# Scan inputs: centred weight, raw input, one variance per image, first taps on ScalarE, products grouped by form

## The reference

```python
xn = (x - x.mean(1)) / jnp.sqrt(x.var(1) + 1e-5) * ln_w + ln_b   # over the 192 channels, per pixel
xz = jnp.einsum('dc,bchw->bdhw', in_proj_w, xn)                  # 384 x 192
xc, z = jnp.split(xz, 2, axis=1)
xc = conv3x3(xc, conv_w, 'SAME', feature_group_count=192)        # depthwise
xc = silu(xc + conv_b)
x_dbl = jnp.einsum('kcd,bkdl->bkcl', x_proj_w, xs)               # xs: xc read in 4 directions; 12 + 4 + 4 rows each
```

## Time and profile before

| | us |
|---|---|
| median of 3 runs | 5882.74 |
| lowest, highest | 5879.74, 5885.18 |
| span of the profiled execution | 5874.6 |
| busy in the span: PE, DVE, ACT, POOL | 5234.5, 4111.9, 2823.1, 805.7 |

### The profile page before, as it was taken

One profiled execution on the slowest core, in us unless ns is written; L12 is line 12 of the kernel. 1 busy time (PEld: TensorE's weight loads), 2 busy tenths in 40 slices (PEclk: granted clock), 3 DMA queues, 4 the chain that ended last, 5 costly groups with the idle time before them and its releaser, 6 DMA issues. The chain is left out here.

```text
span 5874.6 us, 85825 instructions
## 1 busy us (share of the span) xinstructions
PE 5234.5 (89%) x34692; PEld 2383.9 (41%) x34692; DVE 4111.9 (70%) x4899; ACT 2823.1 (48%) x3955; POOL 805.7 (14%) x826
## 2 busy tenths in 40 slices
PE   7799999999989989968869799989778888888879
PEld 2355555555544434445534333333233333333323
DVE  3477677776621122278878499959789999999963
ACT  1144444444432223245521455526587777867844
POOL 1000000000000011122243100000033333323300
PEclk9899999999999989989989899989889999999999
DMA  6522121221032223344433000013300000000034
GB/s 214 138 39 42 22 42 23 40 43 22 15 110 70 81 77 129 111 142 142 132 119 123 29 29 29 33 47 113 99 29 29 5 28 25 16 29 5 17 113 164
DMA packets 298982, 398.22 MB, mean 68 GB/s; under 512 B 143916, under 2 KB 281316, under 8 KB 295324
## 3 DMA queue, kind: packets, MB, share of 16 engines
q1 hardware_dynamic: 271452, 302.90, 17.6%
q0 software_dynamic: 16096, 73.39, 3.7%
q10 hardware_dynamic: 11040, 16.43, 0.9%
HBM read 226.16 MB, written 166.49 MB: 67 GB/s over the span
## 5 line engine op out<-in xcount | busy, mean ns | idle before, releaser
L3884 DVE TENSOR_TENSOR_SCAN s_h<-s_da,s_h 128x448 f32<-128x448 f32 x672 | 729.6, 1124 | 1.5 <-ACT s_da L3811 1.4
L3731 PE MATMUL s_py<-s_prod,s_idf 128*128 128x448 f32 x1344 | 586.6, 559 | 24.5 <-ACT s_ycol L3824 23.3
L622 PE MATMUL b_pc<-b_ca,b_wdm 128*113 128x392 f32 x1152 | 486.9, 520 | 31.9 <-DVE b_wdm L837 25.8
L3811 ACT ACTIVATE s_da<-s_dt,s_al 128x448 f32<-128x448 f32 x672 | 406.1, 658 | 198.3 <-DVE s_h L3884 147.6
L765 ACT ACTIVATE b_band<-b_psel 124x784 f32<-124x784 f32 x264 | 217.7, 825 | 427.5 <-PE b_psel L690 424.4
L622 PE MATMUL b_pc<-b_cb,b_wdm 128*113 128x392 f32 x960 | 403.0, 520 | 0.0
L3869 DVE TENSOR_TENSOR s_h<-s_dtu,s_pb 128x896 f32<-128x896 f32 x336 | 354.9, 1056 | 31.7 <-POOL s_dtu L3918 23.2
L3891 DVE TENSOR_TENSOR s_prod<-s_h,s_pc 128x896 f32<-128x896 f32 x336 | 360.8, 1074 | 0.1
L3907 POOL TENSOR_TENSOR s_dt<-s_dt,s_dtu 128x448 f32<-128x448 f32 x168 | 249.3, 1484 | 782.7 <-DVE s_h L3884 427.5
L2861 DVE SCALAR_TENSOR_TENSOR j_zc<-j_zt,kept_vec,j_zc 128x896 f32<-128x896 f32 x320 | 344.9, 1144 | 6.7 <-ACT j_zt L2803 6.4
L3731 PEld LDWEIGHTS s_py<-s_prod,s_idf 128*128 128x128 f32 x1344 | 249.2, 193 | 220.0 <-issue 167.3
(11 more groups left out here) (726 smaller groups left out, 11252.0 us busy)
## 6 DMA issues: line engine op xcount, KB each, us to landing
b_qk<-mid_qkvp SPq DMA_DIRECT2D x96, 240.2 KB
d_vt<-mid_vd SPq DMA_DIRECT2D x200, 96.0 KB
d_qs<-mid_qd SPq DMA_DIRECT2D x20, 744.0 KB, 5.3
d_ks<-mid_kd SPq DMA_DIRECT2D x20, 744.0 KB, 7.7
b_v<-mid_qkvp SPq DMA_DIRECT2D x6, 1922.0 KB
mid_pout<-d_out POOLq DMA_DIRECT2D x20, 558.0 KB, 4.4
mid_qkvp<-a_out SPq DMA_DIRECT2D x42, 248.0 KB, 2.2
mid_qkvp<-a_out ACTq DMA_DIRECT2D x42, 248.0 KB, 2.1
```

The costliest lines, as they stand in the source:

```text
L622: mm = pe.matmul(pc[n % 2][0:113, 0:392], wdm[:, slot, p, 0:113], src, start=(w == STARTS[a]), stop=(w + 1 == STARTS[a + 1]))
L3731: mm = pe.matmul(y, idf[:, :], prod[j % 3][:, e, :], start=(pr == 0 and e == 0), stop=False)
L3811: last = a.activation(da[j % 4][:, e, :], dt[s % 2][:, span(c)], ACT.Exp, scale=al[:, u, n:n + 1])
L3884: v.tensor_tensor_scan(x, along(da[j % 4][:, e, :]), x, before_, ALU.mult, ALU.add).then_inc(scanned, 1)
```

## The change

- The projection weight is centred once: `column_means` and three additions take the channel mean out of `w` ahead of the loop. So `normal` multiplies the raw input `xin` with `rs`, and the copy `ce` goes. Centring on TensorE stays, for the variance.
- `moment` makes one map per image (two) where there were three tiles, so `root` has two thirds of the elements; `normal` becomes three instructions.
- Tap 0 of the convolution goes from VectorE to ScalarE (`opening`, three instructions), in round s for chunk s-1, behind `inputs(s-2)`.
- TensorE's products of two chunks are interleaved, so that those of one form stand together. `small` takes two whole products with block-diagonal weights (`wtd`, `wbd`) and two pairs of half width; `pB` and the bf16 parts use 128 partitions, of which 64 are stored. `bc_done` is now raised at the end of the round.
- The input buffer is freed by `normed`, not by `centred`.

```diff
+            def column_means():
+                pe.wait_ge(scaled, 3)
+                pe.matmul(pB[:, 0, 0:2 * C], drop[:, :], w[:, 0, :], start=True, stop=False)
+                pe.matmul(pB[:, 0, 0:2 * C], drop[lo, :], w[lo, 1, :], start=False, stop=True).then_inc(column_sums, 1)
...
+            def moment_pair(s):
+                pe.wait_ge(squared, s + 1)
+                pe.matmul(pA[:, 0, 0:CH], m192[lo, :], sq[lo, 1, :], start=True, stop=False)
+                pe.matmul(pA[:, 1, 0:CH], m192[hi, :], sq[hi, 1, :], start=True, stop=False)
+            def moment_full(s):
+                pe.matmul(pA[:, 0, 0:CH], m192[:, :], sq[:, 0, :], start=False, stop=True)
+                pe.matmul(pA[:, 1, 0:CH], m192[:, :], sq[:, 2, :], start=False, stop=True).then_inc(spread, 1)
...
             for s in range(LAST + 1):
                 if live(s):
-                    centre(s)
+                    centre_halves(s)
+                if live(s - 1):
+                    project_halves(s - 1, 0)
+                if live(s):
+                    centre_pair(s)
+                if live(s - 1):
+                    project_pair(s - 1, 0)
+                if live(s):
+                    centre_full(s)
                 if s == 0:
                     biases()
+                    column_means()
                 if live(s - 1):
-                    project(s - 1, 0)
+                    project_full(s - 1, 0)
                 if live(s):
-                    moment(s)
+                    moment_pair(s)
+                if live(s - 1):
+                    project_pair(s - 1, 1)
+                if live(s):
+                    moment_full(s)
                 if live(s - 3):
-                    small(s - 3)
+                    small_full(s - 3)
                 if live(s - 1):
-                    project(s - 1, 1)
+                    project_full(s - 1, 1)
+                    project_halves(s - 1, 1)
+                if live(s - 3):
+                    small_halves(s - 3)
...
             def square(s):
                 a.wait_ge(centred, s + 1)
-                if s >= 2:
-                    a.wait_ge(normed, s - 1)
-                a.activation(ce[s % 2][:, :, :], pA[:, :, 0:CH], ACT.Copy).then_inc(copied, 1)
                 a.activation(sq[:, :, :], pA[:, :, 0:CH], ACT.Square).then_inc(squared, 1)
...
-                a.activation(rs[:, :, :], pA[:, :, 0:CH], ACT.Ln, bias=EPS).then_inc(log_done, 1)
+                a.activation(rs[:, :, :], pA[:, 0:2, 0:CH], ACT.Ln, bias=EPS).then_inc(log_done, 1)
...
+            def opening(s):
+                for t in range(3):
+                    a.activation(img(cv[s % 2][:, t, :]), ct[s % 4][:, t, 0:8, 0:W], ACT.Identity, bias=cb[:, t:t + 1], scale=cw[:, t, 0:1]).then_inc(first_tap, 1)
...
                 if live(s - 2):
                     inputs(s - 2)
+                if live(s - 1):
+                    a.wait_ge(halo_ready, s)
+                    opening(s - 1)
                 if live(s + 1):
                     a.preload_act_table_set("natural_log_exp_and_others")
...
+            v.wait_ge(column_sums, 1)
+            for t in range(3):
+                v.tensor_tensor(w[:, t, :], pB[:, 0, 0:2 * C], w[:, t, :], ALU.add).then_inc(folded, 1)
...
-                        if k == 0:
-                            v.tensor_scalar(dst, tap, cw[:, t, 0:1], cb[:, t:t + 1], ALU.mult, ALU.add).then_inc(tap_done, 1)
+                        if k == 1:
+                            v.wait_ge(first_tap, 3 * s + t + 1)
...
-                v.tensor_tensor(xn[s % 2][:, :, :], ce[s % 2][:, :, :], rs[:, :, :], ALU.mult).then_inc(normed, 1)
+                v.tensor_tensor(x[:, 0:3:2, :], m[:, 0:3:2, :], rs[:, :, :], ALU.mult).then_inc(normed, 1)
+                v.tensor_tensor(x[lo, 1, :], m[lo, 1, :], rs[lo, 0, :], ALU.mult).then_inc(normed, 1)
+                v.tensor_tensor(x[hi, 1, :], m[hi, 1, :], rs[hi, 1, :], ALU.mult).then_inc(normed, 1)
...
                 if live(s - 2):
-                    taps(s - 2, 0, 8)
+                    taps(s - 2, 1, 8)
```

More of the change, by code:

```diff
@@ L2960, in scan_inputs @@
         do = [sb(f"f_do{i}", [128, CH]) for i in range(NO)]
-        rest = sb("f_rest", [64, CH])
-        bo = [sb(f"f_bo{i}", [64, 3, CH], BF16) for i in range(NO)]
+        rest = sb("f_rest", [128, CH])
+        bo = [sb(f"f_bo{i}", [128, 3, CH], BF16) for i in range(NO)]
         pA, pI, pD, pB = pt("f_pa", 3), pt("f_pi", 3), pt("f_pd"), pt("f_pb")
@@ L3068, in _ @@
         def _(pe):
[L3069 to L3079, removed]
+            pe.wait_ge(consts, 2)
             def biases():
@@ L3094, in centre, with centre_pair, centre_full, project_halves @@
                     pe.wait_ge(log_done, s)
[L3095 to L3102 removed]
+                pe.matmul(pA[lo, 1, 0:CH], drop[:, lo], x[:, 0, :], start=True, stop=False)
+                pe.matmul(pA[hi, 1, 0:CH], drop[:, hi], x[:, 2, :], start=True, stop=False)
+            def centre_pair(s):
+                x = xin[s % NX]
+                pe.matmul(pA[:, 0, 0:CH], drop[lo, :], x[lo, 1, :], start=True, stop=False)
+                pe.matmul(pA[:, 2, 0:CH], drop[hi, :], x[hi, 1, :], start=True, stop=False)
+            def centre_full(s):
+                x = xin[s % NX]
+                pe.matmul(pA[:, 1, 0:CH], keep1[:, :], x[:, 1, :], start=False, stop=True)
+                pe.matmul(pA[:, 0, 0:CH], keep[:, :], x[:, 0, :], start=False, stop=True)
+                pe.matmul(pA[:, 2, 0:CH], keep[:, :], x[:, 2, :], start=False, stop=True).then_inc(centred, 1)
+            def moment_pair(s):
+                pe.wait_ge(squared, s + 1)
+                pe.matmul(pA[:, 0, 0:CH], m192[lo, :], sq[lo, 1, :], start=True, stop=False)
[3 more added lines that the diff above has]
+                pe.matmul(pA[:, 1, 0:CH], m192[:, :], sq[:, 2, :], start=False, stop=True).then_inc(spread, 1)
+            def project_halves(s, m):
                 x, base = xn[s % 2], C * m
@@ L3115, in project @@
[L3115 to L3120, removed]
+                mm = pe.matmul(pI[lo, 1, 0:CH], w[:, 0, base + 128:base + 192], x[:, 0, :], start=(m == 0), stop=(m == 1))
@@ new lines, in project_halves, with project_pair @@
+                mm = pe.matmul(pI[hi, 1, 0:CH], w[:, 2, base:base + 64], x[:, 2, :], start=(m == 0), stop=(m == 1))
+                if m == 1:
+                    mm.then_inc(product, 1)
+            def project_pair(s, m):
+                x, base = xn[s % 2], C * m
+                if m == 1:
+                    pe.wait_ge(x_evac, 3 * s + 2)
+                pe.matmul(pI[:, 0, 0:CH], w[lo, 1, base:base + 128], x[lo, 1, :], start=True, stop=False)
+                pe.matmul(pI[:, 2, 0:CH], w[hi, 1, base + 64:base + 192], x[hi, 1, :], start=True, stop=False)
@@ new lines, in project_full @@
+            def project_full(s, m):
+                x, base = xn[s % 2], C * m
+                pe.matmul(pI[:, 0, 0:CH], w[:, 0, base:base + 128], x[:, 0, :], start=False, stop=True).then_inc(product, 1)
+                pe.matmul(pI[:, 2, 0:CH], w[:, 2, base + 64:base + 192], x[:, 2, :], start=False, stop=True).then_inc(product, 1)
+                if m == 1:
+                    pe.wait_ge(x_evac, 3 * s + 3)
+                mm = pe.matmul(pI[:, 1, 0:CH], wd[:, m, :], x[:, 1, :], start=(m == 1), stop=(m == 0))
+                if m == 0:
+                    mm.then_inc(product, 1)
@@ L3124, in small @@
                     pe.wait_ge(dts_evac, s)
+                    pe.wait_ge(rest_done, s)
                 else:
+                    pe.wait_ge(small_ready, 4)
                     pe.wait_ge(bias_ready, 1)
[L3127 to L3136, removed]
+                pe.matmul(pD[:, 0, 0:CH], wtd[:, :], x[:, 1, :], start=True, stop=False)
@@ new lines, in small_full, with small_halves @@
+                pe.matmul(pB[:, 0, 0:CH], wbd[:, :], x[:, 1, :], start=True, stop=False)
+            def small_halves(s):
+                x = xo[s % NO]
+                pe.matmul(pD[lo, 0, 0:CH], wt[:, 0, :], x[:, 0, :], start=False, stop=True)
+                pe.matmul(pD[hi, 0, 0:CH], wt[:, 2, :], x[:, 2, :], start=False, stop=True).then_inc(dts_done, 1)
+                pe.matmul(pB[lo, 0, 0:CH], wbp[:, 0, :], x[:, 0, :], start=False, stop=True)
+                pe.matmul(pB[hi, 0, 0:CH], wbp[:, 1, :], x[:, 2, :], start=False, stop=True).then_inc(bc_done, 1)
```

66 lines of the change are left out of this document (35 added, 31 removed).

## The result

The changed kernel takes 5924.8 us (median of 4 runs, 5924.1 to 5929.9) against 5882.0 for the kernel before on the same chip (4 runs, 5879.7 to 5885.2): a ratio of 1.0074, 95% interval 1.0060 to 1.0089. The forecast was 5923.0, slower with a chance of 0.93. Repeated later on another chip the changed kernel took 5923.6 us, ratio 1.0077 [1.0063, 1.0091].

A forecast was written before the change was run, and what follows sets the result against it. TensorE, busy all 20.63 us of a scan_inputs round, was taken to set the pace. Rounds 2 to 15 go from 277.3 to 315.8 us, plus 2.1 ahead: +40.6, so 5882.7 + 40.6 = 5923 us, range 5906 to 5933.

The forecast's parts named there:

- TensorE's work in a round: TensorE in scan_inputs: 22 units and 5 changes of form, 17.4 us a round, 3.2 less than before.
- `remainder` to first tap: VectorE between rounds waits out ScalarE's middle, table load, gates, inputs and one opening: 6.2 us, doing only low.
- VectorE's loop: VectorE's round through ScalarE's tail: 6.2 tail, 12.70 taps, 2.07 normal, 1.78 last taps, 0.1: 22.9 us against 20.63.
- TensorE's loop at full clock: Last small product through pB copy, remainder, middle, load and gates to projection 5.1, remaining products 16.65: 21.8 us.
- the clock in it: After about 4.2 us idle each round, TensorE restarts at 1.2 GHz and loses 2.1 us, bounds 1.7 and 2.7.
- TensorE's loop with the slow clock: 21.8 + 2.1 = 23.9 us a round, above VectorE's 22.9, so it binds; 23.5 to 24.5 by the bounds.
- rounds 4 to 13: Ten steady rounds of scan_inputs at TensorE's 23.9 us each: 239 us.
- The unit and the change of form: TensorE's price: 0.75 us per whole product or side-by-side pair, about 0.19 us per change of product form.
- the start: Stage start: column_means and additions into w paid by saved moments and square roots; taken as nothing, bounds -1 and +4.
- The third loop: Not in the prediction: remainder, middle, load, gates, projection, moments, root, normal, last taps, back to remainder.
- the second rival: The gap costs more, or stalls appear such as root coming late: rounds 24.5 to 25, 5929 to 5934 us; 13%.
- The faster rival: TensorE's saving arrives if ScalarE's tail is off both loops: VectorE's 17.5 to 18.4 holds, about 5860 us; 3%.

The follow-up runs named there:

- free tail: Changed kernel with opening behind halo; ScalarE's table load and gates ahead of everything waiting for remainder, middle last; VectorE's low behind normal: 5851.2 us, 0.9950.
- small products early: Changed kernel with the half-width small products right behind the whole ones, so bc_done is no longer TensorE's last product: 5915.0 us, 1.0072.
- filler: Changed kernel with five extra pairs of centring products, later overwritten, ahead of centre_halves from the fourth round on: 5920.5 us, 1.0069.
- the opening alone: Kernel before with only tap 0 moved to ScalarE behind inputs, no other part of the change: 5903.7 us, 1.0046.
- ungrouped version: Kernel of free tail with column_means behind the first moments and TensorE's products chunk by chunk again: 5851.1 us, 0.9948.

## Why the prediction was right, step by step

The sign, the mechanism and the size came out as forecast, the size with some luck: one term was 4.7 us too small, and others together 1.3 too large. By its own terms:

| term | predicted | measured |
|---|---|---|
| TensorE's work in a round | 17.4 | 17.49 (free tail) |
| `remainder` to first tap | 6.2 | 6.13 |
| VectorE's loop | 22.9 | 22.83 (small products early; filler) |
| TensorE's loop at full clock | 21.8 | 21.95, in two parts |
| the clock in it | 2.1 (1.7 to 2.7) | 1.65 or 2.25, mean 1.83 |
| TensorE's loop with the slow clock | 23.9 | 23.60 or 24.20, mean 23.78 |
| `normal` | 2.07 | 2.30 (4093.36 to 4095.66) |
| round 2; round 3 | 18.7; 22.9 | 18.84; 22.84 |
| rounds 4 to 13 | 239 | 237.8 |
| rounds 14; 15 | 20.7; 14.5 | 20.52; 14.41 |
| first tap after the stage's start | +2.1 | +6.8 (39.22 to 46.05) |
| whole stage | +40.6 | +44.0 |

*The loops.* The signs that were named are there: VectorE idle 4.23 us ahead of the first tap, released by `opening`, and 0.64 ahead of `low`, together 4.9 (5.5 said, which left out the 0.6 of `remainder` itself); rounds inside 23 to 24.5; TensorE idle 4.25 (4.2 said), released by `gates`, with a granted clock of 0.88 and 0.90 over the two rounds; `remainder` waiting 0.63 us for the copy out of `pB` (about 1 said). That last wait was the test of which loop binds, and the runs confirm the reading: opening VectorE's loop alone changes no steady round, opening TensorE's leaves 22.83. No run has TensorE's loop binding at full clock, but both of its parts are measured: 5.17 us from the end of the last small product to the projection (4097.38 to 4102.55 in the changed kernel) and 16.78 from there (the filler run), together 21.95 where 5.1 + 16.65 was predicted. What is left of 23.60 and 24.20 is the clock, 1.65 and 2.25. The windows give the same loss another way: 0.38 x 4.15 = 1.6 us where the granted clock is 0.62, and 0.48 x 4.85 = 2.3 where it is 0.52.

The steps add up: 20.63 before; 21.99 with the opening alone; 22.84 with `normal` in three pieces too (0.8 us more than before), which is round 3 of the changed kernel, before TensorE has idled that long; 23.78 once TensorE's loop with the slow clock binds.

*TensorE's work.* The unit and the change of form held: 17.49 us with 5 changes, 18.58 with 11. The Trainium skill's page TensorE: Matmul & The Clock Gate (Part 3: Packing small matmuls) has no term for a change of form; by its rule the ungrouped version would need an estimated 16.5 us of TensorE in a round and keep the 17.67 of VectorE. It took 18.58, with TensorE full. So the measurement decides: grouping removes 0.18 us a change. The saving of 3.1 us a round is in the changed kernel too, inside TensorE's loop; it does not shorten the round, because 5.17 us of waiting and 1.83 of slow clock came into the same loop.

*The mis-sized term: the start.* `column_means` and the additions into `w` were taken as nothing, bounded by -1 and +4, on the ground that the moments save as much; that the new order of products could cost something in the fill was not asked. The first tap came 4.7 us later than forecast, above the bound: 2.3 us are lost ahead of the first `normal`, 2.4 behind it. Three rows of TensorE in the first round show the first part:

```profile
3937.74 1.65 PE L3088 MATMUL f_pb<-kept_f_w,f_drop 128*128 128x384 f32 x2 [1.37 <-DVE kept_f_w L3314]
...
3942.38 1.86 PE L3121 MATMUL f_pa<-f_sq,f_m 128*128 128x448 f32 x2
3944.03 1.70 PE L3122 MATMUL f_pa<-f_sq,f_m 128*128 128x448 f32 x2
```

The products of L3088 wait 1.37 us for VectorE's scaling (L3314), the moments are queued behind them, and all of it runs at the slow rate: a moment product, two records, takes 1.65 us (3942.38 to 3944.03), where a round's takes 0.75. The first `normal` starts 25.6 us after the stage's start, before the change 23.3 (3941.28). Moving `column_means` behind the moments gave back 3.1 of it. The second part is the grouped order: the ungrouped version has its first tap 5.3 us earlier. These two together are more than 4.7; that the saved moments and the shorter `root` pay the rest is argued, not shown. The error of +4.7 was partly offset by 1.3 us in the rounds.

*The clock.* Behind every gap of 4.25 us TensorE ran near 1.2 GHz for 3 to 5 us. It cost 1.65 us in seven rounds of ten, just under the lower bound that was taken from the earlier trace rows, and 2.25 in three.

*The third loop* was missed without harm, but by little. At 21.2 us at full clock it lies under the two that were counted; with the 2.25 us of a slow round it would take about 23.5, an estimate, where TensorE's took 24.20. In the three rounds of 24.20 VectorE already waits for `root` ahead of `normal`, once for 0.57 us, the stall that the second rival named:

```profile
4117.57 1.09 DVE L3351 TENSOR_TENSOR f_xn<-f_xin,f_rs 128x896 f32<-128x896 f32 x1 [0.57 <-ACT f_rs L3242]
```

It would have spoiled the forecast of any repair that opens only the two.

*The faster rival* had the right point of decision. With the tail off all loops the kernel took 27 us less than the kernel before on its chip, where the rival's 5860 was 23 less; the round settled at VectorE's work, 17.67, inside its 17.5 to 18.4. What stood against it, the ScalarE order, is what the free tail alters.

## What to carry to other kernels

Where engines pass work round in fixed orders, a round costs its longest closed loop of waits, not the busiest engine: write out for each engine what its last instruction of a round waits for and which first instruction of the next waits behind it, and count every instruction in between. Moving three cheap instructions to an engine with time to spare costs a whole queue if they land behind a wait there; put first what another engine waits for, and last what itself waits. Open all loops before judging work that was taken away: one or two of them opened here gave at most 13.7 us of the stage, all of them 74; and price what is added ahead of a loop at the rate at which the engine runs there, not at the steady one. An order that saves in each round can cost once in the fill: grouping gave 0.9 us a round here and took 5.3 at the start.

## What was not expected of the hardware

After the same gap of 4.25 us TensorE begins some rounds at 2.4 GHz and falls 0.9 us later, and begins others near 1.2 GHz, so the rounds are 23.60 or 24.20; what chooses between them stayed open. After nine gaps of one length, 3.17 us, six rounds began near 1.2 GHz, one fell to it soon after its first products and two stayed at 2.4 GHz; before the change a gap of 2.64 was followed by full rate. And more work made the stage shorter: five extra pairs of products a round, placed in the gap, took 9.9 us off it.
